# First layer of a two-layer attention and expert kernel: three routing steps held back on VectorE, the first projections behind the shared expert, sixteen scatters before expert 0

## The reference, cut to what matters

```
xn = layernorm(x)
x  = x + attention(xn) + ffn(xn)
```

## Time and profile before

| what | us |
|---|---|
| median of 3 runs | 1162.96 |
| their range | 1162.49 to 1164.2 |
| profiled execution, its time | 1164.3 |
| its span, first to last instruction | 1162.5 |
| PE busy in it | 1023.0 |
| VectorE busy | 764.7 |
| ScalarE busy | 605.1 |
| POOL busy | 317.6 |

### The profile page before, as it was taken

The page is one execution under the profiler, slowest core; times in us unless marked ns, Lnnn a source line. Parts: engine busy times, 40 slices in busy tenths (PEclk is TensorE's granted clock), DMA queues, the critical chain, the costliest instruction groups (busy, mean ns, idle before and its releaser), DMA issues.

```text
span 1162.5 us, 17536 instructions
## 1 busy us (share of the span) xinstructions
PE 1023.0 (88%) x5780; PEld 748.4 (64%) x5780; DVE 764.7 (66%) x1591; ACT 605.1 (52%) x911; POOL 317.6 (27%) x331
## 2 busy tenths in 40 slices
PE   4988598568999947699999999999999996999996
PEld 3877576457999943455554555555555555888885
DVE  6585254446665525879889878888888836444438
ACT  6315244346555544256665666666666664544431
POOL 2002678225674430000000021221221000455442
PEclk9999798789999978699999999999999998999999
DMA  6862233244534435111121113222222206333243
GB/s 228 318 268 84 74 128 127 88 129 145 155 119 138 133 148 207 23 28 28 21 36 28 28 48 62 55 55 52 60 64 56 64 23 196 99 103 107 86 186 150
DMA packets 49140, 120.49 MB, mean 104 GB/s; under 512 B 7752, under 2 KB 24904, under 8 KB 48520
## 3 DMA queue, kind: packets, MB, share of 16 engines
q1 hardware_dynamic: 36096, 82.80, 24.9%
q0 software_dynamic: 11808, 32.37, 7.3%
q10 hardware_dynamic: 1152, 4.19, 0.9%
HBM read 72.30 MB, written 52.42 MB: 107 GB/s over the span
## 4 chain that ended last, share of the span: by engine, by line
PE 70%; DVE 16%; issue 4%; ACT 3%; DMA 3%; another core or an unknown queue 2%; POOL 1%; SPq 0%; ACTq 0%; DVEq 0%; POOLq 0%
PE psum L812 10%; PE psum L833 9%; PE psum L821 7%; DVE work_f L1690 6%; PE psum L539 5%; PE psum L541 5%; PE psum L540 5%; PE psum L625 5%; PE psum L626 4%; PE psum L627 4%; PE psum L611 2%; PE psum L636 2%; PE psum L657 1%; DVE x L1305 1%
## 5 line engine op out<-in xcount | busy, mean ns | idle before, releaser
L1690 DVE TENSOR_REDUCE work_f<-psum 128x1 f32<-128x512 f32 x512 | 337.0, 685 | 48.9 <-PE psum L812 46.4
L1198 ACT ACTIVATE work_f<-psum 128x1024 f32<-128x1024 f32 x172 | 169.5, 1024 | 104.9 <-PE psum L821 100.6
L812 PE MATMUL psum<-work_r 128*128 128x512 f32 x512 | 207.6, 444 | 18.7 <-DVE work_f L1690 6.8
L476 POOL DMA_INDIRECT yk<-yb,dest x134 | 131.2, 979 | 239.3 <-ACT yb L1052 207.6
L812 PEld LDWEIGHTS psum<-work_r 128*128 128x128 f32 x512 | 93.4, 190 | 133.5 <-DVE work_f L1690 70.7
L821 PE MATMUL psum<-qm,work_r 128*128 128x512 f32 x512 | 160.8, 396 | 0.9 <-ACT work_f L1198 0.8
L469 POOL DMA_INDIRECT xg<-xn,slot x112 | 108.1, 965 | 181.8 <-PE psum L848 143.4
L821 PEld LDWEIGHTS psum<-qm,work_r 128*128 128x128 f32 x512 | 93.8, 188 | 24.0 <-ACT work_f L1198 6.2
L625 PE MATMUL psum<-wexp,xbh 128*128 x268 | 102.3, 382 | 7.6 <-issue 7.6
L1198 ACT ACTIVATE pt<-psum 128x1024 f32<-128x1024 f32 x84 | 82.8, 1023 | 45.8 <-PE psum L821 42.7
L626 PE MATMUL psum<-wexp,xbh 128*128 x268 | 96.2, 359 | 0.0
(11 more groups left out here) (218 smaller groups left out, 2082.8 us busy)
## 6 DMA issues: line engine op xcount, KB each, us to landing
xb<-xg SPq DMA_DIRECT2D x67, 258.0 KB
xg<-in_pad SPq DMA_DIRECT2D x1, 10320.0 KB
yg<-yk SPq DMA_DIRECT2D x20, 512.0 KB, 9.1
stage<-in_moe SPq DMA_DIRECT2D x16, 608.0 KB
xg<-in_pad SPq DMA_DIRECT2D x1, 7224.0 KB
work_r<-work_r SPq DMA_DIRECT2D x128, 48.0 KB
work_r<-work_r SPq DMA_DIRECT2D x32, 192.0 KB
stage<-in_moe SPq DMA_DIRECT2D x16, 384.0 KB, 4.0
```

Source lines behind the costliest of these rows:

```text
L476: nc.gpsimd.indirect_dma_start(yk[l], bass.IndirectOffsetOnAxis(ap=dest[:, j % 8, i:i + 1], axis=0), yb[l][:, j % 2, i, :], None).then_inc ...
L812: nc.tensor.matmul(next_bank(pe, ("scores", n), b_mx, n + 1), qs[g % 2][:, t * P:(t + 1) * P], km[g % 4][:, r, :], start=True, stop=True). ...
L1198: nc.scalar.activation(pt[((b * NG + g) * QT + t) % 3][:, 2 * h:2 * h + 2, :], psum[:, 3 + 2 * h:5 + 2 * h, :], ACT.Exp, scale=float(HD) * ...
L1690: v.reduce_max(mx[:, s % 2, i:i + 1], ring["scores", n], AX.X).then_inc(b_mx, 1)
```

## The change

VectorE: the routing steps are taken three at a time only from (7, 0) to (9, 0); of the rest, one comes after `hs_lo` of tile 11, one behind the last `add_shared`, one between the second and the third subtract of `projections`, the others behind it. PE: the projections of batch 0 come behind the last down product, in the natural column order. POOL: expert 0's low part stands at n = 16 instead of n = 0.

```diff
-        PROJECTED = (0, 2, 1, 3, 4, 5)
@@ POOL
-            early = {0: 0, 20: 1, 24: 2, 44: 3, 48: 4}
+            early = {16: 0, 20: 1, 24: 2, 44: 3, 48: 4}
@@ PE
-                for n in (PROJECTED if b1 == 0 else range(6))[n0:n1]:
+                for n in range(n0, n1):
                     for i in range(KH):
-                        ins = mm3(psum[:, o0 + n - (n0 // 4) * 4, :], w0_hi[0][:, i, n * P:(n + 1) * P], ...
+                        ins = mm3(psum[:, o0 + n - n0, :], w0_hi[0][:, i, n * P:(n + 1) * P], ...
...
-                if j == B * NFS0 - 1:
-                    pe.wait_ge(f_h, tiles(0, B * NFS0 - 1))
-                    project0(0, 2, 0, 0)
-                    pe.wait_ge(f_h, tiles(0, B * NFS0))
-                    project0(2, 4, 0, 0)
                 shared_down(0, j, NFS0)
+            pe.wait_ge(f_h, tiles(0, B * NFS0))
+            project0(0, 4, 0, 0)
             pe.wait_ge(m_tot, layers(0, 1))
             project0(4, 6, 0, 4)
@@ ScalarE
-                for i, n in enumerate(PROJECTED[:4] if b1 == 0 else range(4)):
-                    act.wait_ge(a_pj, b1 * 6 + i + 1)
+                for n in range(4):
+                    act.wait_ge(a_pj, b1 * 6 + (n + 1))
@@ VectorE
-            def projections(b1, o0):
-                for i, n in enumerate(PROJECTED[:4] if b1 == 0 else range(4)):
-                    dve.wait_ge(a_hi, b1 * 4 + i + 1)
+            def projections(b1, o0, between=lambda n: None):
+                for n in range(4):
+                    dve.wait_ge(a_hi, b1 * 4 + (n + 1))
                     v.scalar_tensor_tensor(out=qk_lo[:, n, :], ...).then_inc(a_lo, 1)
+                    between(n)
...
-                if j >= 7:
+                if (7, 0) <= (j, half) <= (9, 0):
                     for _ in range(3):
                         next(to_slots, None)
+                if (j, half) == (B * NFS0 - 1, 1):
+                    next(to_slots, None)
 
             shared(0, NFS0, routing0)
+            next(to_slots, None)
+            dve.wait_ge(f_y, batches(0, B))
+            dve.wait_ge(s_c, 32)
+            projections(0, 0, lambda n: next(to_slots, None) if n == 1 else None)
             for _ in to_slots:
                 pass
-            dve.wait_ge(f_y, batches(0, B))
-            dve.wait_ge(s_c, 32)
-            projections(0, 0)
```

More of the change, by code:

```diff
@@ L696, in project0 @@
             def project0(n0, n1, b1, o0):
-                for n in (PROJECTED if b1 == 0 else range(6))[n0:n1]:
+                for n in range(n0, n1):
                     for i in range(KH):
-                        ins = mm3(psum[:, o0 + n - (n0 // 4) * 4, :], w0_hi[0][:, i, n * P:(n + 1) * P], w0_lo[0][:, i, n * P:(n + 1) * P],
+                        ins = mm3(psum[:, o0 + n - n0, :], w0_hi[0][:, i, n * P:(n + 1) * P], w0_lo[0][:, i, n * P:(n + 1) * P],
                                   xt_hi[0][:, i, bass.ts(b1, S)], xt_lo[0][:, i, bass.ts(b1, S)], i == 0, i == KH - 1)
```

## The result

| kernel | median us | runs, lowest to highest | ratio [95%] |
|---|---|---|---|
| before | 1164.8 | 20, 1161.99 to 1168.45 | |
| changed | 1161.18 | 20, 1157.47 to 1163.43 | 0.9975 [0.9965, 0.9985] |

The change saves 2.9 us by the ratio (1.7 to 4.1 by its interval), where 7 were forecast. The profiled execution of after has a time of 1159.85 us, a span of 1158.0 and a granted clock of 0.958; against the one of before (1164.3) that is 4.45 less.

A forecast was written before the change was run, and what follows sets the result against it. PE, busy 88% of the span, was taken as the bound. The 5.2 us of the first part plus 1.8 from late results costing less made 7: 1162.96 - 7 = 1156.0 us, range 1147 to 1161.

The forecast's parts named there:

- Routing steps held back; projections behind the shared stage: Shared expert's last tiles: 4.16 us of routing steps leave PE's wait, projections run later in one piece; gain 5.2 us.
- The held steps come back: VectorE before batch 0's attention: the postponed routing steps fit into 2.9 us of slack; cost 0, slots complete at 96.2.
- Sixteen scatters ahead of expert 0: POOL: first scatter 96.9, expert 0 about 117, expert 1 near 134.5, last scatter 203.4 instead of 210.41.
- What the run does to batch 0: Batch 0's attention beside the sixteen scatters: late results until 119.6, values at 132 instead of 138.9; gain 7 us, including 5.2.
- the hold: Attention: PE's results reach ScalarE 8 to 11 us late; tied to POOL's scatter runs by coinciding times, not proved.
- rival A: Attention: late results belong to the attention, not to the scatters; only 5.2 us gained, 1157.8; chance 0.20.
- B: Batch 0: no late results, expert 1 starts at 125.5; gain up to 15.8 us, 1147.2; chance 0.16.
- C: Batch 0: lateness outlasts POOL's 3.7 us scatter pause at expert 0, ends at 128.4; 3.2 us lost, 1166.2; chance 0.10.
- a coincidence of times: Attention: late results end within 4 us of a scatter run's end, seen twice, called no proof.
- The sum: Whole kernel: 7 us off the median 1162.96 gives 1156.0; all behind the first layer's attention moves with it; chance 0.48.

The follow-up runs named there:

- e6d: Changed kernel with POOL's scatter runs cut at eight by low parts and pauses, on chip 7: 1141.07 us, ratio to before 0.9772.
- e3e: Changed kernel with all 64 scatters put behind the attention, on chip 7: 1219.78 us.
- e4: Changed kernel with the low parts of experts 1 and 2 moved back to n = 28 and 32, on chip 2: 1166.1 us, ratio to before 0.9995.
- e6's second form: Changed kernel, scatter runs cut at eight, expert 4 at n = 48, last pause at 56: 1138.82, 1139.34 and 1141.07 us on chips 4, 10 and 7.

## Why the prediction was right and wrong

*Routing steps held back; projections behind the shared stage.* Right: `hs_lo` of tile 11 at 85.89 (86.5 forecast), `cmpb` at 89.57 (90.2), the first matmul of the attention at 98.42 (98.9), 5.7 us earlier than before.

*The held steps come back.* Right: the slots at 95.35 (96.2), nobody late.

*Sixteen scatters ahead of expert 0.* Right: first scatter 96.48 (96.9), expert 0 at 116.66 (117.1), expert 1 at 134.87 after 9.89 (134.5 after 9), last scatter 203.66 (203.4).

*What the run does to batch 0.* Right in mechanism and size: the last late copy at 119.19 (119.6), the value projection at 121.55 (121.6 by the sum), the third batch released at 207.29 (207.2). Two things were luck in part. The end of the hold was carried over from two coincidences, and behind other long runs it comes up to 9 us after the run's end, not 2.6. And when it ended, only two of the four blocks of transposes were done on TensorE (the third starts at 119.36, the fourth at 120.81), not three, which cost nothing, since the fourth waits for the last late copy anyway. The table of runs, e6d and e3e speak against rival A; B and C didn't come, since the hold neither vanished nor outlasted the pause. On chip 12, without a hold, expert 1 came at 124.93, where B had put it (125.5). What I called a coincidence of times was the cause. The weak point was to take the hold as a given of the kernel: it came on some chips only, and there with long runs.

*The sum* is the step that failed: "All that follows the first layer's attention has the same order as before and moves with it." The order did, the time didn't: 6.9 us at the release became 4.5 at the end, and on chip 2 6.2 became 2.8. The sum had no term for what changes behind the attention. Of the 2.4 us of the result some 1.5 lie where TensorE's granted clock is lower over the same matmuls (0.53 against 0.63, 0.73 against 0.86), and 0.6 in the load of tokens that took 5.28 us instead of 4.64; on chip 2 most of the loss lies at 0.88 against 1.00. That is read from four executions, not tested; why the clock falls at other matmuls after the change stays open. A shift of 6 to 7 us at the third batch was worth 3 to 5 at the end.

The distance from 1156.0 to 1161.18 is 5.2 us. 1.8 of it is the base: the sum started from the median of three runs (1162.96), and twenty gave 1164.8. 2.6 is what was lost in the shift (7 to 4.45), and 0.8 lies between the one profiled execution (4.45 less) and the medians (3.6 less).

*What the prediction had no way to see:* on four of the six chips there was no hold at all, and the scatters bound the kernel before; the same change is worth 13.6 us there (chip 12, 0.9881).

*A forecast behind the prediction that failed:* e4, by 8 to 12 us. Its first step held: the twelve scatters beside batch 0's contexts made these late, and expert 1 came at 139.53 (139 expected). What I hadn't counted is the next run of twelve, 151.3 to 166.1: it made batch 1's contexts up to 4.7 us late, so that POOL waited 5.29 us again at expert 3. The last scatter came 1.8 us earlier than in the changed kernel on that chip (202.12 against 203.88), not 3 to 9, and VectorE's addition for the third batch 5.5 us later (213.18 against 207.70).

**The better version.** On chips with late releases it is e6's second form: 1141.07, 24 us below before beside it by the medians and 27 by the ratio, and some 19 below the changed kernel on chip 2, in another group. On the others the changed kernel stays ahead, 1128.71 against 1138.82 and 1139.34 in other groups: three pauses of 3.7 to 6.4 us lie in POOL's chain, and the last scatter comes at 205.5 and 206.4 instead of 194.4. Both beat before on the chips where they were timed. Cutting the runs with useful work instead of pauses wasn't tried.

## What to carry to other kernels

Before you pay a waiting engine's idle time away with indirect scatters, look whether they stand in long unbroken runs beside TensorE's work: with the runs cut at eight the kernel took some 24 us less than before on a chip where they delay TensorE's readers, and some 10 us more than the changed kernel where they don't. When a wait ends "remote" and no row names its releaser, move the suspected transfers alone and see whether the wait goes along. Take a shift in the middle of a kernel at the end only with a discount for what lies behind it (here 2.4 of 6.9 us went, and 3.4 of 6.2), and add it to the time of the execution from which it was worked out.

## What the runs showed of the hardware

- Readers of TensorE's results started up to 11.6 us late beside unbroken runs of twelve to sixteen indirect scatters of 128 rows, one each 1.27 us. Late results begin 5.5 to 12 us into a run; runs of eight leave at most 3.3 us.
- That depends on the chip, or on the time at which it was used: each was met in one group of runs. The same kernel took 1163.5 to 1170.8 us in all 19 runs on chip 2 and 1138.5 to 1145.6 in all runs on chips 12, 13, 4 and 10. What the chips differ in, and where the results wait, no run shows.
- Eight small POOL operations, each waiting for the one before by a semaphore, took 3.7 to 3.8 us, 0.47 each, in ten of twelve pauses, and 6.42 in the last one on chips 4 and 10. Why these two took longer no run shows.
